# Distance attention: tables, first queries and keys loaded during the projections, first tiles spread by VectorE

## What is computed

```
x = x + attn_a(layernorm(x));  x = x + ffn(layernorm(x))
x = x + attn_b(layernorm(x));  x = x + ffn(layernorm(x))

# attn_b, 16 heads of 8:
scores = einsum('bqhd,bkhd->bhqk', q, k) / sqrt(8)
pos_emb = dist_emb[MAX_POS - 1 + (pos_q - pos_k)]
scores = scores + einsum('bqhd,qkd->bhqk', q, pos_emb)
scores = scores + einsum('bkhd,qkd->bhqk', k, pos_emb)
ctx = einsum('bhqk,bkhd->bqhd', softmax(scores), v)
```

## Time and profile before

| | us |
|---|---|
| median of the runs | 4140.59 |
| profiled execution | 4119.65 |
| its span, first to last instruction | 4117.9 |
| projections of layer b and start of distance attention, 2507.8 to 2618.1 | 110.3 |

### The profile page before, as it was taken

One profiled execution on the slowest core, in us unless ns is written; L12 is line 12 of the kernel. 1 busy time (PEld: TensorE's weight loads), 2 busy tenths in 40 slices (PEclk: granted clock), 3 DMA queues, 4 the chain that ended last, 5 costly groups with the idle time before them and its releaser, 6 DMA issues. The chain is left out here.

```text
span 4117.9 us, 71243 instructions
## 1 busy us (share of the span) xinstructions
PE 3405.4 (83%) x27092; PEld 2091.6 (51%) x27092; DVE 3435.6 (83%) x4264; ACT 2880.4 (70%) x2433; POOL 1135.8 (28%) x983
## 2 busy tenths in 40 slices
PE   3899999999999999999947943788888898897990
PEld 2333333333333333333335941687887887887790
DVE  7999999999999999999937545688788787887762
ACT  3999999999999999999803413565666665664530
POOL 2112121122122221112100542534334325330235
PEclk8999999999999999999977976899999999997995
DMA  5000000000000000000032224412213112112122
GB/s 157 7 13 6 13 13 12 7 13 13 6 13 13 6 13 13 6 13 13 5 107 68 65 53 164 65 25 39 40 18 48 31 25 44 28 18 74 27 64 67
DMA packets 237592, 146.43 MB, mean 36 GB/s; under 512 B 147104, under 2 KB 220416, under 8 KB 236832
## 3 DMA queue, kind: packets, MB, share of 16 engines
q1 hardware_dynamic: 228640, 125.03, 12.7%
q0 software_dynamic: 8704, 17.84, 1.8%
HBM read 90.73 MB, written 52.10 MB: 35 GB/s over the span
## 5 line engine op out<-in xcount | busy, mean ns | idle before, releaser
L698 PE MATMUL psA<-wave,diag 128*128 128x512 f32 x3072 | 1441.4, 621 | 137.1 <-DVE score L854 89.3
L766 ACT ACTIVATE wave<-wave 128x2048 f32<-128x2048 int32 x640 | 1181.2, 1904 | 3.6 <-DVE wave L841 2.2
L698 PEld LDWEIGHTS psA<-wave,diag 128*128 128x128 f32 x3072 | 582.8, 196 | 896.2 <-issue 699.8
L635 POOL TENSOR_TENSOR diag<-ident,par 128x128 f32<-128x128 f32 x384 | 291.3, 784 | 1423.8 <-PE psA L698 1423.8
L816 DVE TENSOR_SCALAR wave<-s,par 128x2048 int32<-128x2048 int32 x480 | 617.3, 1286 | 0.0
L841 DVE TENSOR_SCALAR wave<-wave 128x2048 int32<-128x2048 int32 x512 | 613.4, 1227 | 0.0
L1730 POOL COPY kb<-ks 48x1024 bf16<-48x1024 bf16 x160 | 331.1, 2069 | 587.9 <-PE psR L1790 404.0
L1871 ACT COPY r<-psR 128x1024 f32<-128x1024 f32 x320 | 310.7, 1025 | 152.1 <-PE psR L1790 152.1
L1880 ACT ACTIVATE W<-psR 128x1024 f32<-128x1024 f32 x256 | 253.2, 1024 | 167.4 <-PE psR L1815 164.7
L731 ACT ACTIVATE s<-psS,par 128x1024 int32<-128x1024 f32 x256 | 282.8, 1105 | 121.8 <-PE psS L661 121.8
L854 DVE SCALAR_TENSOR_TENSOR score<-wave,par,psA 128x1024 f32<-128x1024 f32 x256 | 318.9, 1281 | 37.0 <-PE psA L698 37.0
(11 more groups left out here) (259 smaller groups left out, 4469.3 us busy)
## 6 DMA issues: line engine op xcount, KB each, us to landing
ks<-kb_parts SPq DMA_DIRECT2D x56, 384.0 KB, 6.2
qs<-qb_parts SPq DMA_DIRECT2D x32, 384.0 KB, 6.3
ys<-f_ys SPq DMA_DIRECT2D x36, 256.0 KB, 2.5
wave_out<-og SPq DMA_DIRECT2D x33, 256.0 KB, 2.1
o<-wave_out SPq DMA_DIRECT2D x8, 1024.0 KB, 5.3
qp<-qa_parts SPq DMA_DIRECT2D x32, 192.0 KB, 3.4
kp<-ka_parts SPq DMA_DIRECT2D x32, 192.0 KB, 3.9
f_wu<-in_w_up SPq DMA_DIRECT2D x2, 2048.0 KB, 11.0
```

The source lines that it names most:

```text
L635: ins = pool.tensor_tensor(diag[:, h % 2, f, :], ident[:], par[:, u, 1, h * NF + f:h * NF + f + 1] .to_broadcast((P, P)), ALU.mult)
L698: mm = pe.matmul(psA[:, kt, :], diag[:, h % 2, f, :], wave[:, h % 2, f, kt * L:(kt + 1) * L], start=(f == 0), stop=(f == PE_F - 1), skip_g ...
L766: act.activation(wave[:, h % 2, f, :], angle[:, h % 2, f, :], ACT.Sin, scale=float(TWO_PI / 2.0 ** 32)).then_inc(sine, 1)
```

## The change

A small class `FirstTiles` now owns `T`, `qs`, `ks` and their counters, and lives around both blocks. The clearing of T, qs and ks moves from VectorE to POOL and into the projections. SP loads T ahead of the first send, the first query and key tile between the sends of batch 5 and batch 6, and the next two key tiles behind the last send. In distance attention POOL clears both key tiles `kb`, and VectorE clears `psDO` and `qb` and makes the first three spreads. POOL makes all the later ones, as before.

```
+class FirstTiles:
+    def __init__(self, c, sb, sem):
+        self.T = sb(c, "T", [ROWS, 2, WIN], BF16)
+        self.qs = sb(c, "qs", [ROWS, 2, 2 * H, P], BF16)
+        self.ks = sb(c, "ks", [ROWS, QT - 1, 2 * H, P], BF16)
...
 # project_block, SP
+            if not wave:
+                sp.wait_ge(near.rows_zeroed, 1)
+                for at in (0, ODD):
+                    sp.dma_start(near.T[at:at + NR, :, at // ODD:WIN],
+                                 dram["t_parts"][:, :, 0:WIN - at // ODD]).then_inc(near.t_loaded, 16)
             for b in range(B):
                 send(b)
+                if not wave and b == B - 3:
+                    for u in range(2):
+                        for s in range(NS):
+                            sp.wait_ge(stored[s][u], each)
+                    sp.wait_ge(near.rows_zeroed, 3)
+                    near.load_tile(sp, near.qs[:, 0, :, :], dram["qb_parts"], 0, 0, near.qs_loaded[0])
+                    near.load_tile(sp, near.ks[:, 0, :, :], dram["kb_parts"], 0, 0, near.ks_loaded[0])
...
+            if not wave:
+                sp.wait_ge(near.rows_zeroed, 6)
+                for t in range(1, QT - 1):
+                    near.load_tile(sp, near.ks[:, t, :, :], dram["kb_parts"], 0, t, near.ks_loaded[t])
...
 # project_block, POOL
+        if not wave:
+            @block.gpsimd
+            def _(pool):
+                pool.memset(near.T[:], 0.0).then_inc(near.rows_zeroed, 1)
+                pool.wait_ge(near.rows_zeroed, 1)
+                pool.memset(near.qs[32:64, 0, :, :], 0.0).then_inc(near.rows_zeroed, 1)
+                for t in range(QT - 1):
+                    pool.memset(near.ks[32:64, t, :, :], 0.0).then_inc(near.rows_zeroed, 1)
+                pool.memset(near.qs[32:64, 1, :, :], 0.0).then_inc(near.rows_zeroed, 1)
...
 # distance_attention, SP
-            sp.wait_ge(rows_zeroed, 1)
-            load_q(0)
-            sp.wait_ge(rows_zeroed, 2)
-            load_k(0)
-            sp.wait_ge(rows_zeroed, 3)
-            for at in (0, ODD):
-                sp.dma_start(T[at:at + NR, :, at // ODD:WIN],
-                             dram["t_parts"][:, :, 0:WIN - at // ODD]).then_inc(t_loaded, 16)
-            for u in (1, 2):
-                sp.wait_ge(rows_zeroed, 3 + u)
-                load_k(u)
-            sp.wait_ge(rows_zeroed, 6)
             load_q(1)
             load_v(0)
...
 # distance_attention, POOL
-            pool.memset(kb[:, 0, :, :, :], 0.0).then_inc(zeroed, 1)
-            pool.wait_ge(zeroed, 2)
-            for kind, i in spreads:
+            for i in range(KB):
+                pool.memset(kb[:, i, :, :, :], 0.0).then_inc(zeroed, 1)
+            pool.wait_ge(kb_ready, 8)
+            for kind, i in spreads[3:]:
...
-                if (kind, i) == ("k", 0):
-                    pool.wait_ge(kb_ready, 4)
-                    pool.memset(kb[:, 1, :, :, :], 0.0).then_inc(zeroed, 1)
-                    pool.wait_ge(zeroed, 3)
...
 # distance_attention, DVE
-            dve.memset(qs[32:64, 0, :, :], 0.0).then_inc(rows_zeroed, 1)
-            dve.memset(ks[32:64, 0, :, :], 0.0).then_inc(rows_zeroed, 1)
-            dve.memset(T[:], 0.0).then_inc(rows_zeroed, 1)
-            dve.memset(qb[:], 0.0).then_inc(zeroed, 1)
-            for i in range(1, KS):
-                dve.memset(ks[32:64, i, :, :], 0.0).then_inc(rows_zeroed, 1)
-            dve.memset(qs[32:64, 1, :, :], 0.0).then_inc(rows_zeroed, 1)
             dve.memset(psO[:], 0.0).then_inc(psO_clear, 1)
+            dve.memset(qb[:], 0.0).then_inc(qb_clear, 1)
+            dve.wait_ge(qb_clear, 1)
+            dve.wait_ge(qs_loaded[0], 32)
+            for half in range(2):
+                spread(dve, qb, qs[:, 0, :, :], half, qb_ready)
+            for u in range(2):
+                dve.wait_ge(zeroed, u + 1)
+                dve.wait_ge(ks_loaded[ks_of(u)], 32)
+                for half in range(2):
+                    spread(dve, kb[:, kb_of(u), :, :, :], ks[:, ks_of(u), :, :], half, kb_ready)
```

More of the change, by code:

```diff
@@ L43 @@
 ODD = 64
+ROWS = ODD + NR
 FRAC = 24
@@ L97, in build @@
         clear_semaphores()
-        project_block(nc, sb, ps, sem, "b", a, X, None, ident, mv, rstd, dram, None, None)
-        distance_attention(nc, sb, ps, sem, a, X, ident, dram)
+        with ExitStack() as c:
+            near = FirstTiles(c, sb, sem)
+            project_block(nc, sb, ps, sem, "b", a, X, None, ident, mv, rstd, dram, None, None, near)
+            distance_attention(nc, sb, ps, sem, a, X, ident, dram, near)
         layer_norm(nc, sb, sem, "lnf2", X, mv, rstd)
@@ L102, in build, with load_tile @@
         last_block(nc, sem, a, X)
+class FirstTiles:
[3 more added lines that the diff above has]
+        self.ks = sb(c, "ks", [ROWS, QT - 1, 2 * H, P], BF16)
+        self.t_loaded = sem(c, "t_windows_loaded")
+        self.qs_loaded = [sem(c, f"qs_loaded{i}") for i in range(2)]
+        self.ks_loaded = [sem(c, f"ks_loaded{i}") for i in range(QT - 1)]
+        self.rows_zeroed = sem(c, "rows_zeroed")
+    def load_tile(self, sp, dst, src, g, t, landed):
+        for at in (0, ODD):
+            sp.dma_start(dst[at:at + NR, :, :],
+                         src[g * 2 * H:(g + 1) * 2 * H, :, t * P:(t + 1) * P]
+                         .rearrange("h r n -> r h n")).then_inc(landed, 16)
 def last_block(nc, sem, a, X):
@@ L157, in _, with project_block @@
             act.activation(root[:], var[:], ACT.Sqrt).then_inc(root_ready, 1)
-def project_block(nc, sb, ps, sem, layer, a, X, V, ident, mv, rstd, dram, params, bound):
+def project_block(nc, sb, ps, sem, layer, a, X, V, ident, mv, rstd, dram, params, bound, near=None):
     wave = layer == "a"
@@ L1502, in _, with distance_attention @@
                     rows_down(i - 2, which[i - 2])
-def distance_attention(nc, sb, ps, sem, a, X, ident, dram):
+def distance_attention(nc, sb, ps, sem, a, X, ident, dram, near):
     PAIRS = P // 2
@@ L1664, in distance_attention @@
         psO_clear = sem(c, "psO_clear")
+        qb_clear = sem(c, "qb_clear")
         o_taken = sem(c, "o_taken")
@@ L1667, in distance_attention, with spread @@
         block = c.enter_context(nc.Block())
+        def spread(engine, dst, src, half, ready):
+            pairs = slice(half * PAIRS // 2, (half + 1) * PAIRS // 2)
+            for odd in range(2):
+                rows = slice(odd * ODD, odd * ODD + NR)
+                engine.tensor_copy(
+                    dst[rows, pairs, odd, :],
+                    src[rows, :, :].rearrange("r h (n two) -> r n h two", two=2)[:, pairs, :, odd]
+                ).then_inc(ready, 1)
         @block.sync
         def _(sp):
-            def load(dst, src, q, t, landed):
-                g = q // QT
-                for at in (0, ODD):
-                    sp.dma_start(dst[at:at + NR, :, :],
-                                 dram[src][g * BH:(g + 1) * BH, :, t * P:(t + 1) * P]
-                                 .rearrange("h r n -> r h n")).then_inc(landed, 16)
             def load_q(q):
@@ L1681, in load_q @@
                     sp.wait_ge(filled, fill["c", (q - 2) * QT + QT - 1, 3] + 1)
-                load(qs[:, q % 2, :, :], "qb_parts", q, q % QT, qs_loaded[q % 2])
+                near.load_tile(sp, qs[:, q % 2, :, :], dram["qb_parts"], q // QT, q % QT, qs_loaded[q % 2])
             def load_k(u):
@@ L1686, in load_k @@
                     sp.wait_ge(filled, fill["c", k_loads[u], 3] + 1)
-                load(ks[:, ks_of(u), :, :], "kb_parts", u // QT, tile_of(u), ks_loaded[ks_of(u)])
+                near.load_tile(sp, ks[:, ks_of(u), :, :], dram["kb_parts"], u // (QT * QT), tile_of(u),
+                               ks_loaded[ks_of(u)])
             def load_v(g):
@@ L1724, in _ @@
         def _(pool):
[L1726 to L1730, removed]
-                        dst[rows, pairs, odd, :],
-                        src[rows, :, :].rearrange("r h (n two) -> r n h two", two=2)[:, pairs, :, odd]
-                    ).then_inc(ready, 1)
             def spread_q(q):
```

23 lines of the change are left out of this document (7 added, 16 removed).

## The result

The changed kernel takes 4158.53 us in the median of 11 runs (4145.25 to 4163.1), the kernel before 4143.94 us in the median of 11. The ratio is 1.0033, with a 95% interval of 1.0021 to 1.0045: 13.7 us slower, between 8.7 and 18.6. The forecast was 11.1 us slower, 4151.7 us. (One run of before took 10128 us and is not compared. The forecast counted from the 4140.6 us of three runs; the median of all of them is 3.3 us higher, which is part of the distance from 4151.7 to 4158.5.)

A forecast was written before the change was run, and what follows sets the result against it. Bounds: VectorE first, the DMA engines in the sends, then a chain of clearing, load and spread. +14.5 + 12.3 - 15.7 = +11.1 us on the 4140.6 us median gave 4151.7 us, range 4137 to 4166.

The forecast's parts named there:

- clearings hold VectorE: Start of layer b's projections: POOL's clearings delay eight normalisations and all VectorE work queued behind them, +14.5 us.
- moved loads: Projections' sends and end: eight query and key tile loads ahead of the barrier open it 12.3 us later.
- start of distance attention: From POOL's first instruction to unit 1's first addition: earlier loads and clearings and VectorE's spreads save 15.7 us.
- values of batch 0: VectorE's additions in the projections, queued behind the statistics: expected at about 2536.6 us, before at 2522.12.
- the two small operations: Two fp32 scalar operations on the variances in the projections: if held as well, the sum would be the same.
- the first boundary: End of a POOL clearing at 2513.3 us: two normalisations through by then, one at each of the next four boundaries.
- the forecast's own bound of 10.6: Lower bound of the clearings' delay in the projections: 10.6 us if two normalisations pass at each boundary.
- The rival that only instructions which read hold VectorE: Projections: POOL's clearings do not hold VectorE, 3.4 us faster, 4137.2 us; chance 0.12.
- The lower bound of 8.8: Barrier behind the projections: only 8.8 us later if the last four loads hide wholly behind it.
- POOL has cleared the first kb by t+3.5 and the second by t+7.1, ahead of their use: Start of distance attention, t being POOL's first instruction there: both key tiles are cleared before they are needed.
- the 1.2 that was taken: Start of distance attention: each of VectorE's twelve spread copies takes 1.2 us, as its maxima of that size, 14.4 together.
- The rival by which VectorE's copies cost as much as POOL's: Distance attention's start: at 1.95 us a copy the saving is 6.7, total 4160.7 us; chance 0.16.

The follow-up runs named there:

- clearings_only: Kernel before plus only six POOL clearings, of the same sizes, of a tile nobody reads at the start of the projections; ratio 1.0037 against before.
- gated: Changed kernel, but POOL clears T at once and each other tile only after the normalisations of batches 2 to 6; ratio 0.999 against before.
- loads_behind: Changed kernel with the first query tile and first three key tiles loaded at the start of distance attention again; ratio 1.0006 against before.
- kb_clear_32bit: Changed kernel with only the two clearings of kb written as 32-bit words; one execution, second addition 18.8 us behind the barrier, marker 30.7.
- pool_spreads: Changed kernel with the first three spreads on POOL again; one execution, second addition 30.1 us behind the barrier, marker (first addition of unit 1) 40.8.
- all_behind_sends: The gated kernel with all eight query and key tile loads behind the last send; one execution, barrier 76.5 us after block start.
- gated_loads_behind: Changed kernel with clearings spaced behind the batches' normalisations and query and key tiles loaded at distance attention's start; ratio 0.9976 against before.

## Why the prediction was right

| term | forecast | in the profiles of before and changed | by the experiments |
|---|---|---|---|
| clearings hold VectorE | +14.5 | +14.5 (values of batch 0: 14.2 to 28.7) | 13.5 at the barrier (clearings_only), 14.8 (gated) |
| moved loads | +12.3 | +12.1 (26.6 at the barrier less 14.5) | 13.1 at the barrier (loads_behind), 11.8 (gated against before) |
| start of distance attention | -15.7 | -13.8 (47.6 to 33.8) | kb_clear_32bit, pool_spreads |
| sum | +11.1 | +12.8 | |

What each of the first two terms costs depends by 1.3 us on whether the other is there; only their sum, 26.6, is read off directly.

The runs' 13.7 us (8.7 to 18.6) agree with 12.8 in the stretch.

**The hold** was the right mechanism with the right length, but the steps inside it were others. The forecast let the two small operations pass in its own sum, then let two normalisations through at the first boundary and one at each of the next four. In the trace the small operations are held, for 3.01 and 2.56 us, and then two normalisations pass at each boundary. The two errors cancel, because either way the last instruction comes with the end of POOL's last clearing. That is luck in part: with two passing at each boundary and the small operations not held, the forecast's own bound of 10.6 would have come out. The rule of the Trainium skill's page "SBUF — State Buffer", section "SBUF: two separate sides", gave the order as it is seen: an operation of VectorE in a two-port mode takes turns with any operation of POOL, one with two inputs in SBUF only with an operation that reads SBUF. The trace agrees: TENSOR_SCALAR is held even on 128 x 8 elements, while the product of two tensors passes a clearing in 0.17 us. The rival that only instructions which read hold VectorE falls with clearings_only.

**The loads** cost about what their transfer takes. At the end of the last send's issue the delay was 22.2 us. Less 14.5 of hold, the four loads in the middle took 7.7 (7.5 in gated, where there is no hold), and 8.8 was the forecast. The four at the end made the way from there to the barrier 4.4 us longer, 7.3 against 2.9, and 3.5 was the forecast. So the term is right to 0.2 us by two errors of 1 us that go opposite ways. The lower bound of 8.8, by which the last four hide behind the barrier, is excluded by these 4.4 us and by all_behind_sends.

**The start** was overestimated by 1.9 us, in the step "POOL has cleared the first kb by t+3.5 and the second by t+7.1, ahead of their use". That asked only when the clearings are needed, and not whom they hold meanwhile, though the forecast had just used that rule one block earlier. VectorE's first copy lost 3.3 us to it. Against that the copies cost 1.05 us and not the 1.2 that was taken, which gives 1.8 back, and the way from the second addition to unit 1 took 11.7 us and not 11.0. These 0.7 us are TensorE's clock: up to 9.1 us behind the second addition both kernels are alike, then the same products take 1.94 us at a share of 0.75 before and 2.60 at 0.54 after.

The rival by which VectorE's copies cost as much as POOL's falls at the prices it named: 1.05 us for 1024 elements, not 1.95. But that is no proof that VectorE does not pay for the 256 bytes between them. The 1.2 was taken from the maxima, and the kernel has faster dense operations from SBUF to SBUF (ns min/median/max; then busy us, mean ns):

```profile
L1377 DVE COPY f_wt<-f_wu x144: 410/418/569, 2282.2 to 4051.9; 128x512 f32 x144
...
L889 DVE TENSOR_SCALAR wave<-wave 128x2048 int32<-128x2048 int32 x512 | 608.2, 1212 | 0.0
```

512 elements in 0.42 us and 2048 in 1.21 make 0.68 us for 1024, an estimate on a straight line between the two; the spread copy takes half as much again. So the rule on 16-byte lines of the Trainium skill's page "SBUF — State Buffer", section "Door 1: The DMA port swizzle", is neither shown nor excluded: no run has VectorE copy the same elements densely, and the type differs too.

**The early T** was free, as said: its two loads went out at 2519.99, 21 us ahead of the first send, and in gated_loads_behind, which has them too, the barrier opens at 62.4 as before.

## What to carry to other kernels

Work given to an idle engine is not free when it shares something with a busy one: look in the trace for a place where the two already ran side by side, and compare the same instruction there and elsewhere. A load moved ahead of a barrier costs its transfer if the DMA engines are busy there, so check their share and not SP's waits: T, moved to where it was 0.13, was free, and eight tiles, moved to where it was 1.02, were not. When single profiles are compared, look at the granted clock of the stretch first; here it was worth up to 1.3 us. Where a moved piece is good for one reason and bad for another, as here, the parts should be made separately: two of them, spaced or put back, turned 13.7 us of loss into 9.9 us of gain.

## What the runs showed of the hardware

- A POOL clearing that reads nothing holds VectorE's TENSOR_SCALAR operations and copies from SBUF to SBUF until it ends, even an operation on 128 x 8 elements (0.17 us alone, 3.01 beside it) and a bf16 copy with 256 bytes between its source elements (1.04 alone, 4.31 beside it). VectorE's reciprocal (0.20), statistics (1.43 for seven), clearings (0.91 and 1.76) and operations on two tensors (0.17) passed beside the same clearings at their usual length.
- A clearing on POOL costs by elements and not by bytes: 3.5 us for 4096 of bf16, 1.8 for the same memory as 2048 words of 32 bits.
- The spread copy of 48 x 1024 strided elements takes VectorE 1.05 us and POOL 1.95.
- The same row of products ahead of the marker, with TensorE busy throughout, takes 1.53 us at a granted clock share of 1.00 and 2.78 at 0.50.
- Loads in pieces of 256 bytes moved 167 to 190 GB/s, and sends queued behind them 384 GB/s where sends alone have 348. This was seen in the table of stretches and not explained.
- At the ends of POOL's instructions two of VectorE's normalisations passed each time in layer b; in layer a two passed at the first and one at each later one. What decides it stays open.
